# Attention and FFN block on one core: the value products of a row tile's own key tile, packed into shared rows

## What is computed

```python
q = (x @ Wq).reshape(2, 512, 32, 128); k = (x @ Wk).reshape(2, 512, 8, 128); v = (x @ Wv).reshape(2, 512, 8, 128)
k = jnp.repeat(k, 4, axis=2); v = jnp.repeat(v, 4, axis=2)        # four query heads share one key head
scores = jnp.where(causal, q @ k.T * 128 ** -0.5, -inf)
probs = softmax(scores, axis=-1)                                  # per batch and head: 512 x 512, lower triangle
x = layernorm(x + (probs @ v) @ Wo)
x = layernorm(x + x @ W_base.T + b_base + experts(x))             # 8 small experts, weights by sparsemax
```

## Time and profile before

| | |
|---|---|
| median of 3 runs | 675.05 us |
| span of the profiled execution, first to last instruction | 673.6 us |
| PE, share of the span | 98% |
| DVE, ACT, POOL | 79%, 62%, 38% |
| transposes on SP's queue | 128, 3.7 us from issue to landing (median) |

### The profile page before, as it was taken

How to read it: one execution, slowest core, us unless ns; L and a number is a source line. 1 busy time by engine, 2 the same in 40 slices (tenths; PEclk the granted TensorE clock), 3 DMA queues, 4 the chain that set the end, 5 groups by cost and what they waited for, 6 DMA issues and landing times.

```text
span 673.6 us, 11403 instructions
## 1 busy us (share of the span) xinstructions
PE 657.9 (98%) x3605; PEld 340.6 (51%) x3605; DVE 531.2 (79%) x1728; ACT 416.8 (62%) x1081; POOL 259.1 (38%) x246
## 2 busy tenths in 40 slices
PE   7899999999999999999999999999999999999996
PEld 3455455455555555455555545455554545455553
DVE  3899778867897688867797688867788578789866
ACT  3796665666556765667566765667556667866331
POOL 1686870166013750166013650167003613352231
PEclk9999999999999999999999999999999999999999
DMA  9357375354914285244924285353835247252602
GB/s 300 139 125 158 74 176 110 65 78 84 239 37 94 49 187 110 54 89 78 231 52 93 48 177 114 49 101 69 201 54 100 49 79 173 56 103 46 111 18 93
DMA packets 200779, 71.80 MB, mean 107 GB/s; under 512 B 169744, under 2 KB 192784, under 8 KB 200720
## 3 DMA queue, kind: packets, MB, share of 16 engines
q1 hardware_dynamic: 199376, 70.04, 48.4%
q10 hardware_dynamic: 1344, 1.05, 0.6%
HBM read 27.02 MB, written 2.10 MB: 43 GB/s over the span
## 4 chain that ended last, share of the span: by engine, by line
PE 89%; DVE 5%; DMA 3%; ACT 1%; POOL 1%; issue 1%; SPq 0%; DVEq 0%; POOLq 0%
PE bank L1259 23%; PE bank L1210 21%; PE bank L1249 15%; PE bank L1234 12%; PE bank L1222 5%; PE bank L1190 4%; PE bank L1291 2%; PE bank L1203 2%; PE bank L1193 2%; DMA pT<-p 2%; DVE p L1065 1%; PE bank L1183 1%; DVE pr L1045 1%; DVE rowmax L946 1%; PE bank L1302 1%
## 5 line engine op out<-in xcount | busy, mean ns | idle before, releaser
L741 POOL TENSOR_SCALAR raw<-raw,scale_of 128x512 f32<-128x512 f32 (+1 forms) x75 | 120.6, 1608 | 315.3 <-ACT wk L807 189.1
L1045 DVE CUSTOM_DVE_ANT_0 pr<-bank,mask,back_of 128x32 f32<-128x32 f32 (+15 forms) x256 | 125.3, 496 | 58.4 <-PE bank L1234 57.6
L863 ACT ACTIVATE pr<-pr,mx 128x288 f32<-128x288 f32 (+15 forms) x256 | 131.0, 512 | 61.2 <-DVE mx L1045 60.3
L1210 PE MATMUL bank<-xT,wq 128*128 128x512 f16 x720 | 164.5, 379 | 0.3 <-DVE y L1082 0.3
L872 ACT ACTIVATE p<-pr,ri 128x32 f16<-128x32 f32 (+15 forms) x256 | 118.4, 511 | 49.7 <-DVE ri L1056 49.5
L1065 DVE SCALAR_TENSOR_TENSOR p<-pr,ri,p 128x448 f16<-128x448 f32 (+15 forms) x256 | 128.4, 545 | 15.9 <-ACT p L872 14.7
L1234 PE MATMUL bank<-kT,qT 128*128 128x32 f16 (+15 forms) x768 | 122.2, 279 | 3.9 <-DVE qT L925 2.4
L1249 PE MATMUL bank<-pT,v 128*128 128x512 f16 x480 | 122.8, 379 | 0.8 <-DMA pT<-p 0.7
L1210 PEld LDWEIGHTS bank<-xT,wq 128*128 128x128 f16 x720 | 70.2, 98 | 82.1 <-DVE y L1082 0.8
L1234 PEld LDWEIGHTS bank<-kT,qT 128*128 128x128 f16 x768 | 67.7, 98 | 62.4 <-issue 3.9
L1259 PE MATMUL bank<-wo_odd,oT 128*128 128x512 f16 x384 | 96.1, 379 | 0.0
(11 more groups left out here) (145 smaller groups left out, 692.3 us busy)
## 6 DMA issues: line engine op xcount, KB each, us to landing
raw<-in_wo SPq DMA_DIRECT2D x32, 256.0 KB, 3.5
raw<-in_wq SPq DMA_DIRECT2D x30, 256.0 KB, 3.9
raw<-in_wk SPq DMA_DIRECT2D x8, 256.0 KB, 4.3
raw<-in_wv SPq DMA_DIRECT2D x8, 256.0 KB, 4.1
y<-in_x SPq DMA_DIRECT2D x1, 2048.0 KB, 13.0
pT<-p SPq DMA_TRANSPOSE x128, 3.7
out<-y SPq DMA_DIRECT2D x8, 256.0 KB, 2.0
pT<-in_xT SPq DMA_DIRECT2D x6, 256.0 KB, 7.7
```

Of the source, the lines that this page charges most:

```text
L741: eng.tensor_scalar(whole, raw_of(name, key), scale[0], None, ALU.mult).then_inc(sems["scaled"], 1)
L863: eng.activation(pr[:, t % 2, h, 0:w], pr[:, t % 2, h, 0:w], ACT.Exp, bias=mx[:, k:k + 1], scale=-1.0, accum_out=rs[:, k:k + 1]).then_inc( ...
L1045: eng.tensor_tensor_reduce(out=pr[:, t % 2, h, 0:w], in0=psum("S", t, h)[:, 0:w], in1=mask[:, 0:w], scale=score_scale(t), scalar=BIG, op0= ...
L1210: made = eng.matmul(out, wq[:, g % 2, w, h, c * 128:(c + 1) * 128], xT[:, x, c, b * 512:(b + 1) * 512], start=c == 0 and w + x == 0, stop= ...
```

## The change

1. `PV` of the own key tile becomes six matmuls in place of three: groups 2 and 3 keep the three half products, each 256 columns wide; group 1 has high-value times low-probability (128 columns), and one matmul of 128 columns in which the high values of 64 keys stand in rows 64 to 127 and the low values of the same keys in rows 0 to 63; group 0 has one matmul of 128 columns for all three half products, 32 rows each, and 32 rows of zeros.
2. `vx` (new, 16 KB a partition) holds the values repacked for those two matmuls. Four DMA copies from SP's queue fill it for each pair of key tiles (`VX`), after `Vp_lo` of both: 16 pairs, 64 copies. The own tile's `PV` waits for the four.
3. The probabilities lie in four parts (group 0 or 2 low, its high, group 1 or 3 high, its low), and groups 0 and 1 have the high half of their own keys twice: one more ACT instruction for each of the two groups in the 48 tiles with `i > 0` (in the other 16 one instruction writes both). The low half of group 0's own keys goes to another place than the rest of its low half: one more DVE instruction in the same 48 tiles.
4. The transpose of `q = 0` leaves out one block of 128 columns: 3, 7, 11 or 15 blocks in place of 4, 8, 12 or 16.
5. In the tables the eight `Vp` steps of a pair of heads are put into the order of their key tiles where they were not; places stay. The diff shows one such line.
6. The memory set aside for DMAs issued from POOL goes down to 1 KB. POOL issues none.

```diff
-        return [("Vp_lo", u // B // 2, 4 * (u % B) + key[1])]
+        return [("Vp_lo", u // B // 2, 4 * (u % B) + j) for j in ((key[1], key[1] ^ 1) if key[1] == key[0] % NI else key[1:])]
...
-    held, given = [], set()
+    held, given, ready = [], set(), set()
+    def low(x):
+        yield x
+        if x[0] == "Vp_lo":
+            ready.add(x)
+            if ("Vp_lo", x[1], x[2] ^ 1) in ready:
+                for n in range(VX_PARTS):
+                    yield ("VX", x[1], x[2] // 2, n)
...
+            yield from low(x)
...
-        yield (name, *key)
+        yield from low((name, *key))
...
-    ("wk", 0), ("Q_lo", 0, 1), ("norm", 0, 0), ("x", 1, 2), ("S", 1, 2), ("fetch", "wq", 1, 0), ("wq", 0, 3), ("Vp", 0, 3), ("exp", 0, 2),
...
+    ("wk", 0), ("Q_lo", 0, 1), ("norm", 0, 0), ("x", 1, 2), ("S", 1, 2), ("fetch", "wq", 1, 0), ("wq", 0, 3), ("Vp", 0, 0), ("exp", 0, 2),
...
-        def probs(t, q):
-            i = t % NI
-            w = 512 * (i + 1)
-            return p16[:, w * i + w * q:w * i + w * (q + 1)]
+        def own_part(t, q, part):
+            w = 128 * (t % NI + 1)
+            at = 4 * w * (t % NI + q) + part * w
+            return p16[:, at:at + 128]
         def halves_of_probs(t, b):
-            both = probs(t, b // 2).rearrange("p (s m n) -> p s m n", s=2, m=2)
-            return [both[:, s, b % 2, 96 - 32 * b:] for s in range(2)]
-        def turned_of(t, j, s):
+            w = 128 * (t % NI + 1)
+            at = 4 * w * (t % NI + b // 2)
+            return [p16[:, at + part * w + 96 - 32 * b:at + (part + 1) * w] for part in ((1, 0) if b % 2 == 0 else (2, 3))]
+        def turned_of(t, j):
             w = 128 * (t % NI + 1)
             two = 2 * (t % 2)
-            x = pT16[:, two:two + 2, 0:4 * w].rearrange("p a (s h n) -> p a s h n", s=2, h=2)
             c = t % NI - j
-            return x[:, :, s, :, c * 128:(c + 1) * 128]
+            return pT16[:, two:two + 2, 0:4 * w].rearrange("p a (s n) -> p a s n", s=4)[:, :, :, c * 128:(c + 1) * 128]
...
+                    c0 = 128 * (1 - q)
...
-                        pT16[:, 2 * (t % 2) + q, 0:cols].rearrange("p (c n) -> p c n", n=128),
-                        probs(t, q)).then_inc(sems[f"turned{q}{t % 2}"], 16)
+                        pT16[:, 2 * (t % 2) + q, c0:4 * w].rearrange("p (c n) -> p c n", n=128),
+                        p16[:, at + c0:at + 4 * w]).then_inc(sems[f"turned{q}{t % 2}"], 16)
+                elif name == "VX":
+                    p, two, n = key
+                    s = v_slot(p, 2 * two)
+                    for tt in (2 * two, 2 * two + 1):
+                        sp_.wait_ge(*done("v_lo", p, tt))
+                    if n == 0:
+                        both = v16[64:128, 0, s:s + 2, :].rearrange("p (a s) n -> p a (s n)", a=1).to_broadcast([64, 2, 512])
+                        eng.dma_start(vx[64:128, :, s:s + 2, :].rearrange("p a s n -> p a (s n)"), both).then_inc(sems[f"vx{p}{two}"], 16)
+                    else:
+                        to, part, of, at = ((0, 1, 1, 64), (0, 0, 0, 96), (32, 0, 1, 96))[n - 1]
+                        eng.dma_start(vx[to:to + 128 - at, part, s:s + 2, :], v16[at:128, of, s:s + 2, :]).then_inc(sems[f"vx{p}{two}"], 16)
...
                         k = 4 * (t % 2) + h
-                        eng.activation(halves_of_probs(t, h)[0], pr[:, t % 2, h, 0:group(t, h)[1]], ACT.Copy,
+                        w, n = group(t, h)[1], 32 * (h + 1)
+                        if q == 0 and w == n:
+                            twice = pr[:, t % 2, h, 0:n].rearrange("p (a n) -> p a n", a=1).to_broadcast([128, 2, n])
+                            own = own_part(t, 0, h + 1).rearrange("p (a n) -> p a n", a=2)
+                            eng.activation(own[:, :, 64 - n:64], twice, ACT.Copy, scale=ri[:, 1, k:k + 1]).then_inc(sems["p_hi"], 1)
+                            continue
+                        if q == 0:
+                            eng.activation(own_part(t, 0, h + 1)[:, 64 - n:64], pr[:, t % 2, h, 0:n], ACT.Copy, scale=ri[:, 1, k:k + 1])
+                        eng.activation(halves_of_probs(t, h)[0], pr[:, t % 2, h, 0:w], ACT.Copy,
                                        scale=ri[:, 1, k:k + 1]).then_inc(sems["p_hi"], 1)
...
                         hi, lo = halves_of_probs(t, h)
                         dve.wait_ge(*done("p_hi", t, h))
-                        made = eng.scalar_tensor_tensor(out=lo, in0=pr[:, t % 2, h, 0:group(t, h)[1]], scalar=ri[:, 1, k:k + 1], in1=hi,
-                                                        op0=ALU.mult, op1=ALU.subtract)
+                        w, n = group(t, h)[1], 0
+                        if h == 0:
+                            n = 32
+                            made = eng.scalar_tensor_tensor(out=own_part(t, 0, 1)[:, 0:32], in0=pr[:, t % 2, h, 0:n], scalar=ri[:, 1, k:k + 1],
+                                                            in1=hi[:, 0:n], op0=ALU.mult, op1=ALU.subtract)
+                        if n < w:
+                            made = eng.scalar_tensor_tensor(out=lo[:, n:w], in0=pr[:, t % 2, h, n:w], scalar=ri[:, 1, k:k + 1], in1=hi[:, n:w],
+                                                            op0=ALU.mult, op1=ALU.subtract)
...
-                    for a, p in half3:
-                        made = eng.matmul(out, v16[:, a, s, cols], turned_of(t, j, p).rearrange('p a m (h n) -> p a m h n', n=32), start=j == 0 and a + p == 0,
-                                          stop=j == i and a == 1)
-                    if j == i:
-                        made.then_inc(sems["PV"], 1)
+                    turned = turned_of(t, j)
+                    hi, lo = turned[:, :, 1:3, :], turned[:, :, 0:4:3, :]
+                    vh, vl = v16[:, 0, s, cols], v16[:, 1, s, cols]
+                    if j < i:
+                        for v, p in ((vh, hi), (vh, lo), (vl, hi)):
+                            eng.matmul(out, v, p.rearrange("p a m (h n) -> p a m h n", n=32), start=j == 0 and v is vh and p is hi, stop=False)
+                    else:
+                        pe.wait_ge(*done(f"vx{g // 2}{2 * b + j // 2}", VX_PARTS - 1))
+                        late = out[:, 1, :, :, :]
+                        eng.matmul(late, vh, hi[:, 1, :, :].rearrange("p m (h n) -> p m h n", n=32), start=j == 0, stop=False)
+                        eng.matmul(late, vh, lo[:, 1, :, :].rearrange("p m (h n) -> p m h n", n=32), start=False, stop=False)
+                        eng.matmul(out[:, 0, 1, :, :], vh, lo[:, 0, 1, :].rearrange("p (h n) -> p h n", n=32), start=False, stop=False)
+                        eng.matmul(late, vl, hi[:, 1, :, :].rearrange("p m (h n) -> p m h n", n=32), start=False, stop=False)
+                        eng.matmul(out[:, 0, 1, :, :], vx[:, 1, s, cols], hi[:, 0, 1, :].rearrange("p (h n) -> p h n", n=32), start=False, stop=False)
+                        eng.matmul(out[:, 0, 0, :, :], vx[:, 0, s, cols], hi[:, 0, 0, :].rearrange("p (h n) -> p h n", n=32), start=False,
+                                   stop=True).then_inc(sems["PV"], 1)
```

More of the change, by code:

```diff
@@ L10 @@
 NV = 16
+VX_PARTS = 4
 TWO15 = 32768.0
@@ L49, in evicted @@
             given.add(x)
-            yield x
+            yield from low(x)
         held = [x for x in held if x not in needed and x != (name, *key)]
-        yield (name, *key)
+        yield from low((name, *key))
         if name == "S":
@@ L112 @@
     ("S", 0, 3), ("S", 1, 0), ("wq", 0, 0), ("S", 1, 1), ("exp", 0, 0), ("most", "o", 0), ("inv", 0, 0), ("exp", 0, 3), ("exp", 1, 1), ("x", 1, 3),
[3 rows of a table removed]
[3 rows of a table added]
     ("fetch", "wq", 1, 2), ("exp", 1, 2), ("exp", 1, 0), ("inv", 1, 0), ("exp", 2, 0), ("wq", 0, 1), ("inv", 1, 1), ("K", 1), ("norm", 1, 0),
     ("exp", 2, 1), ("S", 2, 3), ("factor", "D"), ("exp", 2, 3), ("fetch", "wq", 1, 3), ("norm", 1, 1), ("fetch", "wq", 1, 1), ("exp", 2, 2),
-    ("wo", 0, 2), ("rest", 1, 0), ("Vp", 0, 6), ("inv", 2, 0), ("rest", 1, 1), ("wo", 0, 3), ("S", 3, 0), ("inv", 2, 1), ("Q", 1, 2),
+    ("wo", 0, 2), ("rest", 1, 0), ("Vp", 0, 4), ("inv", 2, 0), ("rest", 1, 1), ("wo", 0, 3), ("S", 3, 0), ("inv", 2, 1), ("Q", 1, 2),
     ("most", "q", 1), ("bits", ("qk", 1)), ("norm", 2, 1), ("S", 3, 1), ("norm", 2, 0), ("rest", 2, 0), ("wo", 0, 1), ("S", 3, 2), ("Q", 1, 0),
     ("exp", 3, 0), ("PV", 0, 0), ("wo", 0, 0), ("rest", 2, 1), ("fetch", "wo", 1, 3), ("exp", 3, 2), ("Q_lo", 0, 0), ("exp", 3, 1), ("Q", 1, 3),
[1 row of a table removed]
[1 row of a table added]
     ("fetch", "wo", 1, 1), ("norm", 3, 0), ("norm", 3, 1), ("S", 4, 1), ("turn", ("qk", 1)), ("PV", 1, 1), ("wq", 1, 2), ("exp", 4, 0),
     ("fetch", "wo", 1, 2), ("exp", 4, 1), ("factor", ("qk", 1)), ("W", 0, 0), ("W", 0, 1), ("fetch", "wv", 1, 0), ("rest", 3, 1), ("S", 4, 2),
[1 row of a table removed]
[1 row of a table added]
     ("wq", 1, 3), ("PV", 2, 0), ("exp", 4, 3), ("W", 1, 0), ("PV", 2, 1), ("exp", 5, 0), ("Q_lo", 0, 3), ("S", 5, 2), ("inv", 4, 1), ("PV", 2, 2),
```

(16 more changed lines are left out.)

## The result

The changed kernel takes 676.6 us (median of 8, 675.1 to 678.0) against 674.95 us of the kernel before in the same session, a ratio of 1.0024 with an interval of 1.0014 to 1.0034. The prediction of 669.0 us (666.0 to 672.8) was wrong in sign. The profiled execution has a span of 675.0 us.

The account below looks back on a forecast made before the run. PE, busy for 98% of the span, was taken as the bound. Of 9.8 us gained, 3.7 us was given back and 6.1 us kept: span 673.6 to 667.5, plus 1.45, about 669.0 us (eight in ten: 666.0 to 672.8).

Parts of the forecast that it names:

- I counted 9.8 us: PE, own key tiles: 648 ns becomes 495 ns, 153 ns less 64 times, the gain if nothing else is late.
- The rival of the weight load: PE: narrow matmuls wait for their weight load, 42 ns each, 677.1 us, or 673.8 at the page's figure; chance 0.05.
- I take nothing: SP's queue: issuing and landing the 64 copies, 0.43 us of issue each, was given no cost in the sum.
- the group stands ahead of the first transpose of a tile with time to spare: SP's queue: places in the other tables are like tile 29, where a 0.7 us push of the transpose does no harm.
- a bound of 11 us: SP's queue: cost from above, 0.7 us for each of 16 copy groups, if every transpose behind were urgent.
- the chain at every tile: Rival: ACT's longer norm also delays O_hi and Q_hi, stalling PE at every tile; around 674 to 680 us; chance 0.09.
- I expect no change there: PE's granted clock: stays at the upper level, 2.4 GHz, as PE never idles long enough to lower it.
- I gave back 3.7 us in all: Whole kernel: losses of 0.6 + 1.3 + 1.0 + 0.8 us taken off the PE gain, leaving 6.1 us.
- no gain in the first four tiles: Start, up to 80 us: DVE, ACT and transposes set the pace, so 4 x 0.15 = 0.6 us of gain is lost.
- the longer chain: norm and rest to PV: added ACT and DVE instructions issue a tile's last transpose up to 0.74 us later; 0.65 taken.
- Tile 31: PV(31,0): 0.5 us of room, short by 0.15 to 0.2 us; the table repeats three times, so 0.6 us.
- the two old waits: PE at 530.16 and 627.11, already waiting for transposes to land: each grows by 0.65 us, 1.3 us together.

Follow-up runs that it names:

- e7_no_extra: e3_none without the two added ACT instructions and the added DVE instruction of a tile, part of the products left out; 665.7 us, ratio 0.9861.
- e9_gaps: Changed kernel, first copy group behind the last wq(1, .) fetch, second behind tile 1's transposes, third behind the last wo(1, .) fetch; 669.4 us, ratio 0.9912.
- e3_none: Changed kernel without any vx copy, products reading unpacked values instead, so a bound and no kernel to use; 667.3 us, ratio 0.9888.
- e4_order: Kernel before with only the changed order of the Vp steps and the evictions that follow, no copies; 674.6 us, ratio 0.9996.
- e2_copies: Kernel before, own arithmetic, plus the 64 copies where the change has them, its Vp order and PV's wait; vx not read; 682.9 us, ratio 1.0119.
- e1_hold: Changed kernel with the first two groups of four vx copies issued behind the last wq(1, .) fetch; 671.6 us, ratio 0.9948.
- e10_before_gaps: Kernel before, own arithmetic, with all 64 copies placed as in e9_gaps, vx not read; 675.15 us, ratio 1.0005.
- e5_hold3: Changed kernel, first copy group behind the last wq(1, .) fetch, second behind tile 2's transposes, third behind tile 3's; 673.5 us, ratio 0.9969.

## Why the prediction was wrong, point by point

**PE: right.** I counted 9.8 us; e7_no_extra, which keeps the count and width of all narrow matmuls, has 9.3 us (8.6 to 10.3 by its interval). The distances are the ones used. PE after, in the own tile of `PV(31, .)`:

```profile
342.87 0.27 PE L1302 MATMUL bank<-pT,v 128*128 128x256 f16 x1
...
343.09 0.22 PE L1304 MATMUL bank<-pT,v 128*128 128x128 f16 x1
343.15 0.27 PE L1305 MATMUL bank<-pT,v 128*128 128x256 f16 x1
...
343.31 0.22 PE L1307 MATMUL bank<-pT,vx 128*128 128x128 f16 x1
343.37 1.47 PE L1266 MATMUL bank<-wv,xT 128*128 128x256 f16 x12
```

From 342.87 to 343.37 it is 0.50 us for six, against the 495 ns of the sum; 128 columns take 50 to 60 ns (343.09 to 343.15). PE has the 3797 matmuls expected. The rival of the weight load is out. The 81 ns that the Trainium skill gives for such a stream (TensorE: Matmul & The Clock Gate, Back-to-back issue gap) do not show here either.

**SP's queue and the copies: the step that failed.** "I take nothing", and "the group stands ahead of the first transpose of a tile with time to spare". I asked of each group only which transpose stands behind it, and checked that at tile 29, in steady state. At the start the weight fetches stand behind it too, and DVE already waits for one of them: before, it was issued at 44.0 us and DVE took it up at 48.17. Three groups of 16 were urgent that way. The place of these three is worth 676.6 - 669.4 = 7.2 us, all the copies as they were placed 9.3, in place of nothing. I had even worked out a bound of 11 us, and then left it out of the range and out of the rivals: the two that ended on the other side (the weight load, the chain at every tile) were other mechanisms. The issue of a copy was also mis-sized: 0.43 us, read from a load of a bias, against 0.65.

**The clock: wrong at the start.** "I expect no change there." After PE's waits of 2.36 us (to 57.68) and 3.13 us (to 61.63) the granted clock falls to the lower level, 1.2 GHz (share of the clock is the column ahead of the last two), and 12 matmuls of 256 columns take 64.17 - 61.63 = 2.54 us where the earlier trace rows have 1.31:

```profile
61.63 2.74 PE L1266 MATMUL bank<-wv,xT 128*128 128x256 f16 x12 [3.13 <-DVE qT L962]
```

```profile
60.00:64.00 4.00, 2.37 (x12) 1.68 (x13) 3.65 (x10) 2.42 (x8) 0.00 (x0) 0.50 1.04 198
64.00:68.00 4.00, 4.00 (x30) 2.57 (x29) 2.99 (x15) 3.59 (x9) 0.00 (x0) 0.65 0.57 169
```

At most 2.37 x 0.50 + 4.00 x 0.35 = 2.6 us of the loss come from this. It follows the waits and goes with them: in e9_gaps the clock is 1.00 from 40 to 80 us. The 0.96 ahead of 40 us is no part of it, since e3_none shows 0.96 there too.

**The start, and the chain: too dear.** I gave back 3.7 us in all, of which 0.6 us was no gain in the first four tiles and 3.1 us the longer chain; e7_no_extra prices the chain at 1.6. ACT's part in it was mis-sized: in `norm(31,0)` the two added instructions put the next ones back by 0.21 and 0.23 us (starts at 330.77 and 330.98, 331.52 and 331.75), 0.44 us where I had 0.54, and ACT is busy for 438.0 us in all, not near 443. DVE's 541.0 is as expected. Tile 31 was right in its place: PE waits there for the transpose, once, 0.30 us. The three matmuls ahead should end their turn at 341.12 + 0.65 = 341.77, so the stall is 0.46 us where I had 0.2.

```profile
341.12 0.81 PE L1297 MATMUL bank<-pT,v 128*128 128x512 f16 x3
342.23 0.81 PE L1297 MATMUL bank<-pT,v 128*128 128x512 f16 x3 [0.30 <-DMA pT<-p]
```

But tiles 15 and 47 show no such wait. And the two old waits, which I let grow by 1.3 us, are gone: from 80 to 560 us the wait above is the only one of PE for a transpose, and where I expected PE to wait 2 to 4 us for transposes from 80 us on, it waits 0.3, or 1.4 with the wait at `PV(63,0)` below. It was not the new order (e4_order still has two such waits, 0.8 us), and it does not take the narrow matmuls or the shorter transpose (e2_copies, with those of before, has none from 80 us on). Why they went, no run tells.

**The tail: not foreseen.** Behind 563.6 us the changed kernel falls back from level to 1.6 us late at `PV(63,0)` (637.80 against 636.21), with two new waits of 1.1 us each, both in the list of PE's waits above: the `turn` of `ffn` waits for `rowpower`, for which the last `wb` fetch lands later (POOL starts on it at 572.00 us, before at 570.57), and `PV(63,0)` comes late. The list names only "issue" for the second, but SP issues the last transpose at 631.79 and it lands 5.9 us later, at 637.7. The first is in e3_none as well (1.3 us), so it is not the copies'. The second is not in e3_none. The last two transposes land in 6.1 us (median of the two), before in 4.4, in e3_none in 4.5, in e1_hold in 5.9, in e10_before_gaps in 4.5. Why only the changed matmuls together with copies have it stays open. e9_gaps has it too, with a wait of 0.86 us at `PV(63,0)`: part of the 2.1 us that are left between e9_gaps and e3_none. Another 1.3 us stand between the two profiled executions already at the `S` of 384 columns (41.16 and 39.90 us), and e9_gaps issues its first copy only at 45.08. So the copies in their new places account for little of it; whether the 1.3 us is chance in these two executions, no run shows.

**The forecast took the copies as harmless** and gave 669.0 us; e9_gaps, where they nearly are, has 669.4. That is partly luck, two errors that cancel: without copies e3_none gives back 9.8 - 7.6 = 2.2 us where I had 3.7, and e9_gaps has 2.1 us more than e3_none, of which my sum had nothing.

## What to carry to other kernels

When steps are added to a queue that issues in order, list for each place everything that stands behind it, fetches as well as transposes, and for each the time until its consumer needs it; do so for the start of the program and not only for one place in steady state. A bound that was worked out for an unknown cost belongs in the range, and a mechanism whose bound exceeds the gain is a rival. If a change gives back all that it should gain, compare the start of the same instruction in both traces along the span: here that told at once a gain of 0.15 us a tile from a single loss of 7.8 us.

## What the runs showed of the hardware that I had not expected

A plain copy from SBUF to SBUF held SP's queue for 0.67 to 0.73 us at 64 x 1024 elements and for 0.59 to 0.61 us at 64 x 512 and 32 x 512 (the changed kernel; 4 of its 64 copies took 1.0 to 1.5 us). The issue of one and the same transpose took very different times. The one of `rest(3, 1)` took 1.32 us before, when the fetches ahead were issued 3 us earlier, and 3.64 us in e5_hold3, where it follows them at once:

```profile
63.03 1.32 SPq L690 DMA_TRANSPOSE pT<-p  x1
```

```profile
62.37 0.43 SPq L703 DMA_DIRECT2D raw<-in_wv  x1
63.31 3.64 SPq L723 DMA_TRANSPOSE pT<-p  x1
```

It took 3.47 us in e1_hold and 3.68 in the changed kernel, where it follows fetches too, and 1.35 in e9_gaps with a gap of 3 us ahead of it. So a late fetch can delay the transposes behind it by more than its own issue. It is no rule: right behind the three `wq` fetches at 44.66 a transpose took 1.61 us before, and what makes the difference was not tested. And the clock fell to 1.2 GHz after PE had waited 2.36 us up to 57.68 and 3.13 us up to 61.63, while in e9_gaps, with no wait of PE over 0.7 us from 40 to 82 us, it stayed at 2.4 GHz.
